# The slot table's one-hot matmuls with their operand sides exchanged, and a transpose behind them

## The chip, the cores and the metric

The kernel runs on one core of a Trainium2 chip: TensorE (matmuls), VectorE, ScalarE, GpSimd, SyncE (which issues most transfers) and 16 DMA engines. The metric is the device time of one execution in microseconds. The kernel before took 620.72 us in the median of three runs (619.73 to 621.04).

## What is computed

A small vision model: patches of 64 images become 37 tokens of 192 values each, an attention layer with relative positions is added, then a mixture of eight experts. The change lies in the routing ahead of the experts. Cut to what matters there:

```python
logits = xf @ Wg
topv, topi = jax.lax.top_k(logits, K)               # two experts for each token
w = jax.nn.softmax(topv, axis=-1)
order = jnp.argsort(-w[:, 0])                       # best first
e_ids = topi[order].reshape(T * K)
oh = jax.nn.one_hot(e_ids, E, dtype=jnp.int32)
pos = (jnp.cumsum(oh, axis=0) * oh).sum(-1) - 1     # place in the expert's list
keep = pos < cap
slot = jnp.where(keep, e_ids * cap + pos, E * cap)
buf = jnp.zeros((E * cap + 1, C), xf.dtype).at[slot].set(xf[tok_rep])
h = gelu(einsum('ecd,edh->ech', buf_e, W1) + b1)
out = einsum('ech,ehd->ecd', h, W2) + b2            # then weighted and added back to its token
```

There are 64 x 37 = 2368 tokens and 8 experts with room for 740 rows each. The kernel does not sort. It finds, for each expert, which tokens are in and where, and writes a **slot table**: for each of 8 x 6 tiles of 128 slots, which token sits in each slot. The rows of the tokens are then gathered by that table.

## The kernel before

Tokens are held as 22 groups (NG) of 111 partitions (G, three images of 37). The kernel has an image stage, an attention loop over pairs of groups, the routing stage (some 60 us, about 370 to 430 us in the trace), and a loop over the eight experts. There is no planner: each engine runs its own list in written order, and engines wait for one another by counting semaphores.

The end of the routing stage, with the lines of the profile:

- VectorE finds for each token and each of its two choices (j runs over 2 x 22 = 44 such columns) the tile and the row in the tile. L1632 makes `dest` (111 partitions x 48 tiles x 44, fp16): the token's number (its sign and an offset keep it in fp16) at the tile that it goes to, else 0. L1639 makes `onehot` (111 x 128 rows x 44, fp16) in two halves of 22 j each: 1 at the row in the tile. In both, j is the innermost dimension, so the values that belong to one j stand 44 elements apart. Each of the three instructions raises the semaphore `s_hot` by one.
- TensorE, L963, adds 44 matmuls in one PSUM bank. For each j, `onehot[:, :, j]` is the stationary side (111 x 128) and `dest[:, :, :, j]` the moving side (111 x 48). The sum is the table, 128 rows x 48 tiles, and the last matmul raises `s_tab`. A matmul with j below 22 needs only the first half of the one-hots.
- VectorE, L1644 to L1651, seven small steps on 128 x 48 values, turns the table into `gid`, the row number of each slot as an integer, and `valid`. L1651 raises `s_gid`.
- GpSimd, L1841, waits for `s_gid` and issues the indirect gathers of six tiles for expert 0 (`xe`), then those of expert 1 and 2.
- TensorE, behind the table, waits for `s_gid`, runs ten filler matmuls (`keep_warm`, L784, 128 x 128 by 512 columns, whose results are not used), then transposes each gathered tile as it lands (L974) with fillers between, and starts expert 0 (L1010). Another 20 fillers stand between the matmuls of L954, which count tokens, and L963.

In the trace `onehot`, `dest`, `tid` and `tvoid` are named `narrow`, and `tneg` and `tfold` are named `wide`, by the memory that they are cut from. `PS` is PSUM.

Of the kernel before, what the change touches and what calls it, by code (L numbers as in the profile page):

```python
# [23 lines left out]
E, HID = 8, 4 * D  # L24
# [22 lines left out]
NT = -(-CAP // 128)  # L47
# [51 lines left out]
def tile_rows(i):  # L99
    return min(128, CAP - 128 * i)  # L100


def build(nc, x, ln1_g, ln1_b, W_lin, b_lin, ln2_g, ln2_b, pos_embedding, cls_token,
# [7 lines left out]
    with ExitStack() as ctx:  # L111
        def sb(name, shape, dt=F32):
            return ctx.enter_context(nc.sbuf_tensor(name, shape, dt))
# [7 lines left out]
        def sem(name):  # L121
            return ctx.enter_context(nc.semaphore(name))

        PS = ctx.enter_context(nc.psum_tensor("PS", [128, 8, 512], F32))

        ident = sb("ident", [128, 128])
# [43 lines left out]
        def carve(memory):  # L170

            at = [0]

            def piece(parts, n, dt=F32):
                words = n if dt is F32 else n // 2
                a, at[0] = at[0], at[0] + words
                assert at[0] <= memory.shape[1]
                v = memory[0:parts, a:a + words]
                return v if dt is F32 else v.bitcast(dt)
            return piece  # L180
# [3 lines left out]
        piece = carve(wide)  # L184
        wraw = piece(128, 3 * NQKV).rearrange("p (b n) -> p b n", b=3)
        piece = carve(wide)
# [10 lines left out]
        piece = carve(wide)  # L197
# [4 lines left out]
        piece = carve(wide)  # L202
# [77 lines left out]
        piece = carve(narrow)  # L280
# [7 lines left out]
        piece = carve(narrow)  # L288
        onehot = piece(G, 2 * NG * 128, FP16).rearrange("p (n j) -> p n j", n=128)
# [3 lines left out]
        junk_a = piece(128, BY_ACT * G, BF16)  # L293
        mp_act = piece(128, BY_ACT * G)
        tid = piece(128, E * NT)
        tvoid = piece(128, E * NT)
        dest = piece(G, 2 * NG * E * NT, FP16).rearrange("p (e n j) -> p e n j", e=E, n=NT)

# [113 lines left out]
        s_hot = sem("slot_one_hots_ready")  # L412
        s_tab = sem("slot_table_psum")
# [27 lines left out]
        def bc(ap, shape):  # L441
            return ap.to_broadcast(shape)
# [201 lines left out]
        def _(pe):  # L644
# [4 lines left out]
            for c in range(PC):  # L649
                last = pe.matmul(PS[:, 6, 0:D], meanw[:, :], W_cen[:, c, :], start=(c == 0), stop=(c == PC - 1))  # L650
# [130 lines left out]
            def keep_warm(n, bank):  # L781

                for _ in range(n):
                    pe.matmul(PS[:, bank, 0:512], sums_to[:, 0, :], sums_to[:, 1:5, :].rearrange("p l m -> p (l m)"),  # L784
                              start=True, stop=True, skip_group_check=True)
# [123 lines left out]
            for m in range(HB):  # L909
                last = pe.matmul(PS[:, 6, m * R:(m + 1) * R], wrk[:, m * 128:(m + 1) * 128], pos_f[:, :],  # L910
                                 start=(m == 0), stop=(m == HB - 1), skip_group_check=True)
# [40 lines left out]
            for g in range(NG):  # L952
                one = ab[:, g:g + 1, :, :].rearrange("p a c e -> p a (c e)")
                last = pe.matmul(PS[0:G, 7, (g + 1) * width:(NG + 1) * width].rearrange("p (a c) -> p a c", c=width),  # L954
                                 onesb[:, :], bc(one, [G, NG - g, width]), start=False, stop=True,
                                 skip_group_check=True)
# [3 lines left out]

            for j in range(2 * NG):
                pe.wait_ge(s_hot, 2 + j // NG)
                last = pe.matmul(PS[:, 0, 0:E * NT], onehot[:, :, j], dest[:, :, :, j].rearrange("p e n -> p (e n)"),  # L963
                                 start=(j == 0), stop=(j == 2 * NG - 1))
            last.then_inc(s_tab, 1)
            def first_rows():

                pe.wait_ge(s_gid, 1)
                keep_warm(10, 7)
                for i in range(NT):  # L970
                    pe.wait_ge(s_one[i], 16)
                    n = tile_rows(i)
                    for k in range(2):
                        last = pe.transpose(PS[:, 2 * k + i // 4, 128 * (i % 4):128 * (i % 4) + n],  # L974
                                            xe[0:n, 0, i, k * 64:k * 64 + 128], ident[0:n, 0:n])
                    if i < NT - 2:
                        keep_warm(2, 7)
                last.then_inc(s_xep, 1)
                keep_warm(7, 7)
# [35 lines left out]
            def results(e):  # L1015
# [6 lines left out]
                for i in range(NT):  # L1022
# [14 lines left out]
                    last.then_inc(s_yp, 1)  # L1037

            first_rows()
            hidden(0, True)  # L1040
            expert_rows(1, 1, 0, 0)
# [203 lines left out]
        def _(dve):  # L1245
            v = nc.vector

            def ch(ins):

                dve.drain()  # L1250
# [28 lines left out]
            for c in range(PC):  # L1279
                last = v.tensor_scalar(W_cen[:, c, :], W_raw[:, c, :], g1[:, c:c + 1], None, ALU.mult)  # L1280
# [18 lines left out]
            for c in range(PC):  # L1299
                last = v.tensor_tensor(W_cen[:, c, :], W_cen[:, c, :], PS[:, 6, 0:D], ALU.subtract)  # L1300
# [339 lines left out]
                                bc(inrow[:, at].rearrange("p (a j) -> p a j", a=1), [G, 128, NG]), ALU.is_equal  # L1640
                                ).then_inc(s_hot, 1)
            dve.wait_ge(s_tab, 1)
            tab = PS[:, 0, 0:E * NT]
            ch(v.tensor_scalar(tneg[:, :], tab, -1.0, 0.0, ALU.mult, ALU.max))  # L1644
            v.tensor_scalar(tfold[:, :], tab, 0.0, float(FOLD), ALU.is_lt, ALU.mult)
            v.scalar_tensor_tensor(tvoid[:, :], tab, 0.0, slot_no[:, :, :].rearrange("p e n -> p (e n)"),
# [74 lines left out]
            with dve.Fori(0, E // 2 - 1) as i:  # L1721
                for p in (1, 0):
                    e = i * 2 + 2 - p
# [219 lines left out]
```

## Time and profile before

| | |
|---|---|
| median of three runs | 620.72 us (619.73 to 621.04) |
| the profiled execution | 620.7 us, its span 618.9 us |
| busy share of the span | TensorE matmul 88%, weight load 81%, VectorE 70%, ScalarE 42%, GpSimd 35% |
| mean granted TensorE clock | 0.939 of full speed (2.4 GHz) |
| the 44 table matmuls | 407.95 to 413.14 us |
| gid ready, first expert product | 414.58 us, 428.77 us |

The span is the time from the first to the last instruction of the program; the execution holds 1.8 us more around it. The busy shares are means over stages that are bound by different things, so they don't tell what the routing stage waits for. That is read from the chain of waits and the timeline of that stage. A matmul's duration in the trace holds its way through the array, which overlaps with the next one's, so the cost of one in a burst is the distance between starts. A granted clock of 0.50 is 1.2 GHz, and 1.00 is 2.4 GHz.

### The profile page before, as it was taken

How to read it: one execution, taken by the hardware profiler on the slowest of the kernel's cores; microseconds unless marked ns; L12 is line 12 of the kernel's file. 1: busy time of each engine (PE TensorE's matmuls, PEld its weight loads, DVE VectorE, ACT ScalarE, POOL GpSimd, SP SyncE). 2: the span in 40 equal slices, each digit the busy share in tenths (PEclk: the TensorE clock that was granted, in tenths of full speed). 3: DMA queues.
4: the chain of work that ended last, by engine and by line, in shares of the span. 5: the costliest groups of instructions: out<-in, count | busy, mean ns of one | idle time of the engine just before them, and what ended most of it. 6: DMA issues, size and time to landing. Idle time of an engine off the chain costs nothing.

```text
span 618.9 us, 12396 instructions
## 1 busy us (share of the span) xinstructions
PE 542.4 (88%) x4284; PEld 503.6 (81%) x4284; DVE 433.4 (70%) x1008; ACT 258.8 (42%) x415; POOL 218.2 (35%) x206
## 2 busy tenths in 40 slices
PE   4998477999999999999999796667999999999983
PEld 4997377989989999899899673344899999999982
DVE  6669676476776776777867757662778777777853
ACT  1333333242542443434425205402765685595560
POOL 0247320112012021021120105018587787787364
PEclk9999788799999999999999757869999999999997
DMA  8978632201202102112012008505375475466250
GB/s 198 227 170 246 171 80 63 46 14 39 51 0 51 34 16 51 26 25 51 11 39 51 2 4 226 141 1 134 82 165 134 94 170 136 92 145 149 21 166 32
DMA packets 61978, 54.96 MB, mean 89 GB/s; under 512 B 29174, under 2 KB 52534, under 8 KB 61152
## 3 DMA queue, kind: packets, MB, share of 16 engines
q1 hardware_dynamic: 52799, 46.04, 29.4%
q0 software_dynamic: 9152, 8.59, 8.3%
q8 instruction: 14, 0.23, 0.2%
q14 instruction: 13, 0.10, 0.1%
HBM read 39.32 MB, written 18.27 MB: 93 GB/s over the span
## 4 chain that ended last, share of the span: by engine, by line
PE 44%; DVE 13%; ACT 12%; issue 10%; SPq 9%; DMA 5%; POOL 3%; DVEq 2%; POOLq 0%; ACTq 0%
PE PS L1035 7%; PE PS L726 6%; PE PS L749 6%; ACT wide L1077 4%; PE PS L705 4%; PE PS L1033 4%; ACT hTh L1219 3%; PE PS L733 2%; DVE hTl L1686 2%; PE PS L742 2%; PE PS L740 2%; PE PS L741 2%; PE PS L1010 2%; SPq L496 2%; ACT b2w L1225 2%
## 5 line engine op out<-in xcount | busy, mean ns | idle before, releaser
L1737 POOL TENSOR_TENSOR rs<-ve,nhalf 111x1 f32<-111x1 f32 (+2 forms) x37 | 24.7, 668 | 276.4 <-DVE ve L1333 197.3
L1867 POOL DMA_INDIRECT running_sums<-ye,gid x42 | 73.4, 1747 | 34.8 <-DVE ye L1710 25.6
L1035 PE MATMUL PS<-w2hl,hTh 128*128 128x384 f32 (+1 forms) x288 | 82.8, 357 | 0.0
L1033 PE MATMUL PS<-w2hl,hTl 128*128 128x192 f32 (+1 forms) x288 | 73.5, 255 | 4.0 <-DVE hTl L1686 4.0
L1841 POOL DMA_INDIRECT xe<-routed_rows,gid x48 | 53.3, 1111 | 42.7 <-DVE gid L1651 28.5
L1010 PE MATMUL PS<-xeT,w1h 128*128 128x370 f32 x288 | 64.2, 331 | 2.1 <-issue 1.4
L1686 DVE TENSOR_TENSOR hTl<-hf,hTh 128x740 fp32r<-128x740 f32 x48 | 44.6, 928 | 24.7 <-ACT hTh L1219 23.5
L1033 PEld LDWEIGHTS PS<-w2hl,hTl 128*128 128x128 f32 (+1 forms) x288 | 53.7, 186 | 6.4 <-issue 5.6
L705 PE MATMUL PS<-xT,wh 128*128 128x222 f32 x264 | 46.8, 287 | 7.7 <-DVE xT L1347 7.7
L1035 PEld LDWEIGHTS PS<-w2hl,hTh 128*128 128x128 f32 (+1 forms) x288 | 52.9, 184 | 0.5
L1010 PEld LDWEIGHTS PS<-xeT,w1h 128*128 128x128 f32 x288 | 50.4, 188 | 2.8 <-issue 1.8
L1010 PE MATMUL PS<-xeT,w1l 128*128 128x370 f32 x192 | 48.0, 331 | 0.0
L705 PEld LDWEIGHTS PS<-xT,wh 128*128 128x128 f32 x264 | 37.7, 198 | 9.9 <-issue 9.8
L1216 ACT ACTIVATE hf<-PS,b1s 128x740 f32<-128x740 f32 x48 | 42.1, 877 | 6.3 <-PE PS L1010 3.9
L726 PE MATMUL PS<-wide 111*111 111x96 f32 x336 | 39.8, 283 | 1.0 <-DVE wide L1486 1.0
L674 PE MATMUL PS<-narrow 128*128 128x192 f32 x216 | 38.3, 328 | 2.7 <-ACT narrow L1060 2.5
L726 PEld LDWEIGHTS PS<-wide 111*111 111x111 f32 x336 | 37.9, 196 | 2.0 <-DVE wide L1486 1.1
L1365 DVE SCALAR_TENSOR_TENSOR wide<-PS,ind,wide 111x296 f32<-111x296 f32 x64 | 33.6, 525 | 6.1 <-DMA wide<-rel_scores 2.1
L674 PEld LDWEIGHTS PS<-narrow 128*128 128x128 f32 x216 | 34.7, 190 | 3.4 <-ACT narrow L1060 2.8
L705 PE MATMUL PS<-xT,wl 128*128 128x222 f32 x176 | 34.6, 279 | 0.0
L740 PE MATMUL PS<-woh,oTh 128*111 128x192 f32 x126 | 33.5, 266 | 0.9 <-DVE oTl L1395 0.9
L1090 ACT CAST oTh<-PS 128x666 fp32r<-128x666 f32 x21 | 15.1, 719 | 45.4 <-PE PS L733 45.4
(241 smaller groups left out, 1288.0 us busy)
## 6 DMA issues: line engine op xcount, KB each, us to landing
wide<-x SPq DMA_DIRECT2D x24, 288.0 KB, 13.3
w1r<-L_ffn_W SPq DMA_DIRECT2D x16, 384.0 KB, 4.9
rel_scores<-wide SPq DMA_DIRECT2D x66, 73.0 KB
w2r<-L_ffn_W SPq DMA_DIRECT2D x8, 576.0 KB, 4.6
w1r<-L_ffn_W SPq DMA_DIRECT2D x16, 192.0 KB, 4.5
wide<-rel_scores SPq DMA_DIRECT2D x22, 111.0 KB, 2.3
out<-running_sums SPq DMA_DIRECT2D x1, 1776.0 KB, 7.6
h_tokens<-narrow SPq DMA_DIRECT2D x24, 72.0 KB, 1.9
```

Source lines behind the costliest of these rows:

```text
L674: last = pe.matmul(PS[:, 4 + u % 4, 0:D], xTt[:, u % 2, c, :], W_cen[:, c, :], start=(c == 0), stop=(c == PC - 1))
L705: last = pe.matmul(PS[:, bank, (m % 2) * G2:(m % 2 + 1) * G2], lhsT, xT[:, b_, :], start=(nth == 0 and m % 2 == 0), stop=(nth == len(BLOCK ...
L726: last = pe.matmul(heads(4 - 2 * g, V)[:, j, :], pT[:, g, j * G:(j + 1) * G], v_sb[:, g, h * V:(h + 1) * V], start=(j % HB == 0), stop=Tru ...
L740: pe.matmul(PS[0:G, g, 0:D], oTh[:, g, at], woh[:, c, :], start=(c == 0), stop=False)
L749: last = pe.matmul(PS[0:G, 2 * g + n, 0:HB * V], xT[:, b_, g * G:(g + 1) * G], (wh, wl)[w][:, b_, at:at + HB * V], start=(nth == 0), stop= ...
L1010: last = pe.matmul(PS[:, hidden_bank(c) + n, 0:HALF], (w1h, w1l)[hl][:, b_, w], xeT[:, b_, n * HALF:(n + 1) * HALF], start=(nth == 0), sto ...
L1033: pe.matmul(PS[0:n, bank, 0:D], hTl[:, c, at], w2hl[:, c, 0, :], start=(c == 0), stop=False, skip_group_check=True)
L1035: last = pe.matmul(PS[0:n, bank, 0:2 * D], hTh[:, c, at], both(w2hl[:, c, :, :]), start=False, stop=(c == HC - 1), skip_group_check=True)
L1216: last = nc.scalar.activation(hf[:, c % 2, :].rearrange("p (a n) -> p a n", a=2), src, ACT.Gelu, bias=b1s[:, p, c:c + 1])
L1686: v.tensor_tensor(hTl[:, c, :], hf[:, c % 2, :], hTh[:, c, :].bitcast(F32), ALU.subtract).then_inc(s_hl, 1)
L1841: p_.indirect_dma_start(xe[0:r, p, n, :], None, xr_dram, bass.IndirectOffsetOnAxis(ap=gid[0:r, e, n:n + 1], axis=0), bounds_check=B * T - ...
L1867: p_.indirect_dma_start(sums, at, ye[0:r, e % 2, n, :], None, bounds_check=B * T + NT * 128 - 1, oob_is_err=True, compute_op=ALU.add).then ...
```

## The change

The two sides of the 44 matmuls are exchanged. `dest[:, :, :, j]` (111 x 48) is stationary and `onehot[:, :, j]` (111 x 128) is moving, so the table comes out as 48 partitions x 128 columns in bank 0. VectorE copies it to a new tile `tab_rows` (48 x 128, fp32) and raises `s_hot` to 4. TensorE waits for that and transposes `tab_rows` into bank 2, as 128 x 48, and raises `s_tab` to 2. VectorE waits for that, and its seven steps read bank 2 in place of bank 0. `tab_rows` is named `narrow` in the profile. Nothing else differs, but for the line numbers, which rise by 1 to 5.

```diff
+        tab_rows = piece(E * NT, 128)
...
             for j in range(2 * NG):
                 pe.wait_ge(s_hot, 2 + j // NG)
-                last = pe.matmul(PS[:, 0, 0:E * NT], onehot[:, :, j], dest[:, :, :, j].rearrange("p e n -> p (e n)"),
+                last = pe.matmul(PS[0:E * NT, 0, 0:128], dest[:, :, :, j].rearrange("p e n -> p (e n)"), onehot[:, :, j],
                                  start=(j == 0), stop=(j == 2 * NG - 1))
             last.then_inc(s_tab, 1)
+            pe.wait_ge(s_hot, 4)
+            pe.transpose(PS[:, 2, 0:E * NT], tab_rows[:, :], ident[0:E * NT, 0:E * NT]).then_inc(s_tab, 1)
...
             dve.wait_ge(s_tab, 1)
-            tab = PS[:, 0, 0:E * NT]
+            v.tensor_copy(tab_rows[:, :], PS[0:E * NT, 0, 0:128]).then_inc(s_hot, 1)
+            dve.wait_ge(s_tab, 2)
+            tab = PS[:, 2, 0:E * NT]
```

TensorE's list around the table, before (`sums_to` is what the fillers read, `xe` the gathered rows):

```order
L954 MATMUL PS<-wide,onesb 111x32
L954 MATMUL PS<-wide,onesb 111x16
L784 MATMUL PS<-sums_to 128x512 x20
L963 MATMUL PS<-narrow 128x48 x44
L784 MATMUL PS<-sums_to 128x512 x10
L974 MATMUL PS<-ident,xe 128x128 x2
```

and now:

```order
L955 MATMUL PS<-wide,onesb 111x32
L955 MATMUL PS<-wide,onesb 111x16
L785 MATMUL PS<-sums_to 128x512 x20
L964 MATMUL PS<-narrow 48x128 x44
L968 MATMUL PS<-ident,narrow 128x48
L785 MATMUL PS<-sums_to 128x512 x10
L977 MATMUL PS<-ident,xe 128x128 x2
```

The table's output turned from 128x48 to 48x128, and one transpose stands between it and the ten fillers.

VectorE's list from `dest` to the fourth of the seven steps, before:

```order
L1632 TENSOR_TENSOR narrow<-narrow,wide 111x2112
L1639 TENSOR_TENSOR narrow<-narrow,wide 111x128x22 x2
L1644 TENSOR_SCALAR wide<-PS 128x48
L1645 TENSOR_SCALAR wide<-PS 128x48
L1646 SCALAR_TENSOR_TENSOR narrow<-PS,slot_no 128x48
L1648 TENSOR_SCALAR valid<-PS 128x48
```

and now:

```order
L1635 TENSOR_TENSOR narrow<-narrow,wide 111x2112
L1642 TENSOR_TENSOR narrow<-narrow,wide 111x128x22 x2
L1646 COPY narrow<-PS 48x128
L1649 TENSOR_SCALAR wide<-PS 128x48
L1650 TENSOR_SCALAR wide<-PS 128x48
L1651 SCALAR_TENSOR_TENSOR narrow<-PS,slot_no 128x48
L1653 TENSOR_SCALAR valid<-PS 128x48
```

One copy of 48x128 stands between the one-hots and the seven steps.

## Rows read from the trace of the kernel before

**Rows 1.** Chain of waits, 405 to 430 us: start, us, engine and line.

```profile
406.36 1.55 DVE narrow L1639
...
407.95 5.19 PE PS L963 x44
...
413.17 0.21 DVE wide L1644
...
414.36 0.22 DVE gid L1651
...
415.51 0.33 POOL xe L1841
...
422.86 2.61 DMA xe<-routed_rows,gid
...
428.77 1.24 PE PS L1010 x6
```

**Rows 2.** Who waited for whom, 404 to 430 us: total us, times, longest.

```profile
POOL xe L1841 <- DVE gid L1651: 28.5, 1, 28.5
```

**Rows 3.** One line, L963: duration ns min/median/max, first and last start us.

```profile
L963 PE MATMUL PS<-narrow x44: 302/304/306, 408.0 to 412.8; 111*128 111x48 f16 x44
```

**Rows 4.** Timeline of TensorE's matmuls, 362 to 370 us: start, duration in us.

```profile
363.51 0.39 PE L741 MATMUL PS<-wol,oTh 128*111 128x192 f32 x1
...
366.49 0.39 PE L742 MATMUL PS<-woh,oTl 128*111 128x192 f32 x1
366.68 0.36 PE L898 MATMUL PS<-woh,oTh 128*37 128x192 f32 x1
...
369.40 0.36 PE L900 MATMUL PS<-woh,oTl 128*37 128x192 f32 x1
```

**Rows 5.** Busy us by engine in stretches; behind POOL granted clock, DMA share, GB/s.

```profile
363.30:366.60 3.30, 3.30 (x18) 3.30 (x19) 1.32 (x7) 0.00 (x0) 0.00 (x0) 0.50 0.00 0
366.70:369.50 2.80, 2.80 (x19) 2.73 (x18) 1.05 (x4) 0.00 (x0) 0.55 (x1) 0.50 0.00 0
397.20:400.40 3.20, 3.20 (x20) 2.10 (x19) 0.96 (x4) 0.45 (x1) 0.00 (x0) 0.50 0.00 0
400.60:404.00 3.40, 3.40 (x16) 1.37 (x14) 3.02 (x8) 0.00 (x0) 0.00 (x0) 1.00 0.01 2
404.10:407.20 3.10, 0.00 (x0) 0.00 (x0) 3.02 (x3) 0.00 (x0) 0.00 (x0) 1.00 0.00 0
407.40:413.20 5.80, 5.18 (x44) 4.92 (x44) 2.06 (x3) 0.00 (x0) 0.00 (x0) 0.50 0.02 3
414.65:417.50 2.85, 2.85 (x7) 1.01 (x8) 2.46 (x3) 0.00 (x0) 1.81 (x1) 0.50 0.00 0
417.60:425.50 7.90, 4.70 (x22) 1.83 (x20) 0.00 (x0) 0.00 (x0) 6.48 (x7) 1.00 0.25 66
```

**Rows 6.** Groups of instructions, VectorE, whole span: busy us, mean ns, idle before.

```profile
L1306 DVE COPY cB<-PS 128x192 f32<-128x192 f32 x1 | 0.4, 352 | 0.0
...
L1644 DVE TENSOR_SCALAR wide<-PS 128x48 f32<-128x48 f32 x1 | 0.2, 208 | 3.7 <-PE PS L963 3.7
```

**Rows 7.** One line, L888, columns as in rows 3.

```profile
L888 PE MATMUL PS<-ident,wide x6: 298/298/321, 361.4 to 362.0; 37*128 37x37 f32 x6
```

**Rows 8.** One line, L733, 360.1 to 361.3 us, columns as in rows 3.

```profile
L733 PE MATMUL PS<-ident,wide x6: 390/393/446, 360.1 to 361.1; 111*128 111x111 f32 x6
```

**Rows 9.** Chain of waits, 394.3 to 396.3 us, columns as in rows 1.

```profile
394.62 0.17 DVE last_in L1605
...
394.84 0.38 PE PS L945
...
395.24 0.34 DVE wide L1610
```

**Rows 10.** One line, L784, 400.6 to 403.9 us, columns as in rows 3.

```profile
L784 PE MATMUL PS<-sums_to x16: 379/379/431, 400.4 to 403.7; 128*128 128x512 bf16 x16
```

**Rows 11.** One line, L1639, columns as in rows 3.

```profile
L1639 DVE TENSOR_TENSOR narrow<-narrow,wide x2: 1620/1620/1621, 406.3 to 407.8; 111x2816 f16<-111x2816 f16 x2
```

## The prediction

> **What bounds the kernel now.** I read the chain of waits first, since a change of a few matmuls counts only if it lies on what ends last. In the routing stage the chain runs in one line: VectorE makes the first half of the one-hots (406.36), TensorE runs the 44 table matmuls from 407.95 for 5.19 us, VectorE takes the table at 413.17 and has the gather indices (gid) at 414.36, GpSimd gathers the routed rows from 415.51, the last gather's transfer runs from 422.86 for 2.61, and the experts' first product starts at 428.77 [rows 1]. The reader should see that no other engine stands between these steps. The view of who waited for whom says the same from the other side: GpSimd sat idle for 28.5 us until gid [rows 2]. So a microsecond on the way from one-hots to gid is a microsecond of the whole time.
>
> Then I read what one of the 44 matmuls costs. A single one lasts 304 ns, the first starts at 408.0, the last at 412.8 [rows 3]; the chain's 5.19 us less 0.304 for the last, over 43 steps, is **0.1136 us a step** (0.112 from the rounded starts). The moving side is 48 columns, the stationary side 128. To see which of the two sets the step I took a place in the trace where the stationary width changes and the moving width does not: with 111 stationary columns and 192 moving, 16 steps go from 363.51 to 366.49, 0.186 us each; with 37 stationary and the same 192 moving, 17 steps go from 366.68 to 369.40, 0.160 each [rows 4], both at a granted clock of 0.50 [rows 5]. So a wide stationary side sets the step, and with a narrow one the moving side does, at 0.160/192 = 0.833 ns a column, which is the 1.2 GHz level. In the table matmuls 48 moving columns would be 0.040 us by that price; the step of 0.1136 is the load of 128 stationary columns, 0.887 ns each.
>
> **The change, part by part.** *The 44 matmuls.* Stationary goes from 128 to 48 columns: 48 x 0.887 = 0.043 us. Moving goes from 48 to 128: 128 x 0.833 = 0.107 us. The larger sets the step: 0.107. The burst is then 43 x 0.107 + 0.31 = 4.91 us against 5.19, **-0.28**. What is moved streams through the array in a step nearly as long as the load that it replaces, so little is won. Both tiles keep 44 values side by side for each column, so neighbours in a column sequence lie 88 bytes apart, before and after. The trace has no wide moving operand of that kind. Its cost is bounded from above by the 48 columns that now hide in 0.1136 us, 2.37 ns a column, which would make a step of 0.303 and a burst of 13.3 us (+8.2); from below by the steps at the upper clock, where 512 moving columns go at (403.7 - 400.4)/15 = 0.22 us [rows 10], 0.055 for 128 (the nearest row of a stream without a stationary bound). The nearest row to it is the stationary side of these same matmuls, read with the same 88 bytes at 0.887 ns a column: 0.1136 a step, which saves nothing. I take 0.107 to 0.114, and 0.107 for the sum.
>
> Here a rule speaks against the change. The trace shows 0.887 ns for a stationary column 88 bytes apart, against the 0.833 of a moving column without gaps [rows 3, 4], 6% more. The Trainium skill (Advanced Engine Details and Errata, SBUF Cachelines) says that reads that touch a different 16-byte line each time pay a penalty, and names no figure. By that rule 128 such columns on the moving side could cost more than the 48 did; by the row they cost 6% more at most. I go by the row and keep the rule as a rival below.
>
> *The copy.* VectorE copies 48 partitions x 128 columns out of PSUM. A pass over 48 PSUM columns takes 208 ns, a copy of 192 columns 352 [rows 6]: 1 ns a column, so 128 columns are 0.29 us. It is on the path, before it nothing can start. The handover from TensorE to it is the one that L1644 has today.
>
> *The transpose.* One fp32 transpose, stationary 48 x 128, moving 48. The nearest row is the 37 x 128 one at the same clock, 321 ns for the longest of its run [rows 7]; 111 x 128 took 446 at most [rows 8], and a lone 128 x 111 one with 128 moving 0.38 in the chain [rows 9]. I take 0.34 and keep 0.32 to 0.45. The handovers around it are read from that lone transpose: VectorE's result at 394.62 + 0.17, TensorE's start at 394.84, its end at 395.22, VectorE's next at 395.24 [rows 9], 0.05 and 0.02. Behind TensorE's new wait are queued only the ten filler matmuls and the expert transposes, which wait for gid and the gathers anyway; on VectorE the whole gid computation waits, which is the path itself.
>
> Added together: 0.29 + 0.05 + 0.34 + 0.02 = **+0.70**, bounds 0.68 to 0.81. The rest (seven small VectorE steps, now read from another PSUM bank, and the gathers) keeps its cost.
>
> *The sum.* The profiled execution took 620.7 us (span 618.9 and 1.8 around it), the median of the three runs is 620.72, so both bases agree. 620.7 - 0.28 + 0.70 = **621.1**. With a step of 0.1136 and the longer transpose it is 621.5. A measurement of this kernel can tell about 0.2%, 1.24 us, from no change; the forecast lies inside that.
>
> **Rivals.** *The clock rises in the burst.* Granted TensorE clock was 0.50 (1.2 GHz) for all of 407.4 to 413.2. It had been 1.00 (2.4 GHz) from 400.6 to 407.2 and fell after TensorE had done nothing from 404.1 on; in 397.2 to 400.4 and in 414.65 to 417.5 wide matmuls ran back to back at 0.50, and the stretch behind each has 1.00 [rows 5]. The 5.2 us of 48-column matmuls did not bring it up; 128 moving columns fill nearly the whole step and might. If it rises 2.9 us after the start, as it did for the filler that began at 414.65, 27 of the 44 are done and 17 save 0.107 - 0.055 each, 0.88 us in all: 621.1 - 0.9 = 620.2. If it did not fall at all ahead of the burst, the second half of the one-hots, ready at 407.8 + 1.62 = 409.4 [rows 11], holds matmul 23 back, and the burst ends about 410.9, 2.2 us earlier: 620.7 - 2.2 + 0.7 = 619.2. Against it: the copy and the transpose remain, and one burst of this kind in the trace stayed at 0.50.
>
> *The strided moving side is slow.* This ends on the other side. If each moving column takes two steps of the 1.2 GHz clock, 1.67 ns, a step is 0.213 and the burst 43 x 0.213 + 0.31 = 9.5 us: +4.3 + 0.7, 625.7. It decides from a step of 0.126 us on, where the loss passes 1.24 us. For it: no row shows a wide moving operand with gaps. Against it: the stationary read with the same gaps at 0.887 ns.
>
> *It isn't on the path.* If something else released the gathers within a fraction of a microsecond of gid, the sum would vanish: 620.7. The 28.5 us of idle GpSimd [rows 2] speak against it.
>
> **How the numbers follow.** Forecast (step 0.107 to 0.114, clock at 0.50) 0.60; clock higher in some of the burst 0.20; slow moving side 0.13; off the path 0.07. Slower by over 0.2%: 0.13 and a tail of the forecast, 0.05, together 0.18. Faster by over 0.2% needs the whole burst at the upper level, a quarter of the second case, 0.05. Within: 0.77. The range runs from 619.8 (most of the clock case) to 622.5 (the forecast's bounds and the spread of the runs shown, 1.3 us), and leaves out the slow stream and the fastest clock case.
>
> **What would show it.** In the profile after: the starts of the first and last table matmul 4.6 us apart; a 48 x 128 copy of about 0.29 us; one transpose of 0.32 to 0.45; gid about 0.4 us later behind the one-hots than now (8.00 us from 406.36 to 414.36), and the gathers later by the same. A first-to-last distance over 5.4 us makes the moving side the culprit; under 4 us with a clock above 0.50 is the second case. If the steps are as said and the time still moves by over 1.24 us, the path behind gid is where I was wrong.

## The result, and the profile after

The changed kernel took **629.58 us** (median of 6 runs, 627.14 to 632.05) against 620.55 of the kernel before (6 runs, 619.73 to 621.04): a ratio of 1.0147, interval 1.0122 to 1.0173, some 9 us slower. The forecast was 621.1, inside the range of no change.

The loss sits in one place. The chain of waits of the changed kernel, with the same columns as [rows 1]:

```profile
407.45 1.26 DVE narrow L1635
408.71 1.55 DVE narrow L1642
...
410.30 13.13 PE PS L964 x44
...
423.46 0.29 DVE narrow L1646
...
423.80 0.35 PE PS L968
...
424.17 0.21 DVE wide L1649
...
425.36 0.22 DVE gid L1656
...
426.52 0.33 POOL xe L1846
...
433.86 2.62 DMA xe<-routed_rows,gid
...
439.79 1.95 PE PS L1013 x10
```

The 44 matmuls take 13.13 us where they took 5.19. Everything behind them is as forecast: 0.29 for the copy, 0.35 for the transpose, 0.05 and 0.02 for the handovers, and the seven steps, the gathers and the expert's start keep the distances of [rows 1]. GpSimd's wait for gid is 10 us longer than in [rows 2], though this profile's routing stage also began later. Who waited for whom:

```profile
POOL xe L1846 <- DVE gid L1656: 38.5, 1, 38.5
```

To compare profiles whose routing stages start at different times I use the distance from the start of dest to the end of gid. Before, dest starts at 405.10:

```profile
405.10 1.26 DVE narrow L1632
```

and gid ends at 414.36 + 0.22 [rows 1], so 9.48 us. Now it is 425.58 - 407.45 = 18.13, **8.65 us more**: 13.13 - 5.19 = 7.94 for the burst, 0.71 for copy, transpose and handovers. On 620.55 that makes 629.2, and 629.58 was measured. (The profiled execution itself is the longest of the six, 632.05: it reached dest 2.3 us later than the one before did.)

One matmul of the burst and the two new steps, as in [rows 3] (duration ns min/median/max, first and last start, shapes):

```profile
L964 PEld LDWEIGHTS PS<-narrow x44: 167/178/190, 410.3 to 422.6; 111*48 111x48 f16 x44
L964 PE MATMUL PS<-narrow x44: 482/483/504, 410.3 to 422.9; 111*48 111x128 f16 x44
```

```profile
L1646 DVE COPY narrow<-PS x1: 283/283/283, 423.5 to 423.5; 48x128 f32<-48x128 f32 x1
```

```profile
L968 PE MATMUL PS<-ident,narrow x1: 339/339/339, 423.8 to 423.8; 48*128 48x48 f32 x1
```

A step is (422.9 - 410.3)/43 = **0.293 us**, for 128 moving columns 2.29 ns each. Before it was 0.1136 for 48 moving columns, 2.37 ns each. By the moving side's price the two steps agree; by the price that the prediction used (0.833 ns a moving column, the rest the load) they don't.

The clock is no part of the loss. Stretches of the changed kernel, as in [rows 5]:

```profile
397.20:401.00 3.80, 3.80 (x23) 3.47 (x24) 0.00 (x0) 1.19 (x2) 0.00 (x0) 0.50 0.00 0
...
406.60:410.20 3.60, 0.11 (x1) 0.00 (x0) 3.53 (x4) 0.00 (x0) 0.00 (x0) 1.00 0.00 0
410.40:423.30 12.90, 12.90 (x44) 7.63 (x44) 1.38 (x1) 0.00 (x0) 0.00 (x0) 0.50 0.01 1
```

The burst ran at 0.50 (1.2 GHz), as before; the clock had been 1.00 while TensorE did next to nothing from 406.6 to 410.2, and fell as the burst began. The 12.9 us in which matmuls were always in flight did not bring it back.

### The profile page after: what moved, and what is told of

It reads as the page before. It is cut to its first block, busy times and chain, and to the rows that moved or that the text cites. A ratio compares the mean times of both kernels' runs of the same rounds, so it can differ in the third digit from the quotient of the medians.

```text
span 630.1 us, 12399 instructions
## 1 busy us (share of the span) xinstructions
PE 557.1 (88%) x4285; PEld 511.8 (81%) x4285; DVE 433.6 (69%) x1009; ACT 258.8 (41%) x415; POOL 218.3 (35%) x206
## 4 chain that ended last, share of the span: by engine, by line
PE 45%; DVE 13%; ACT 12%; issue 10%; SPq 10%; DMA 5%; POOL 3%; DVEq 2%; POOLq 0%; ACTq 0%
PE PS L1038 7%; PE PS L727 6%; PE PS L750 6%; ACT wide L1080 4%; PE PS L706 4%; PE PS L1036 4%; ACT hTh L1222 3%; PE PS L734 2%; PE PS L964 2%; PE PS L741 2%; PE PS L743 2%; PE PS L742 2%; SPq L497 2%; DVE hTl L1691 2%; PE PS L1013 2%
## 5 line engine op out<-in xcount | busy, mean ns | idle before, releaser
L675 PE MATMUL PS<-narrow 128*128 128x192 f32 x216 | 39.7, 337 | 2.6 <-ACT narrow L1063 2.6
L675 PEld LDWEIGHTS PS<-narrow 128*128 128x128 f32 x216 | 36.4, 198 | 2.8 <-ACT narrow L1063 2.8
L1013 PEld LDWEIGHTS PS<-xeT,w1l 128*128 128x128 f32 x192 | 34.1, 188 | 0.0
```

Of the source, the lines that this page charges most:

```text
L675: last = pe.matmul(PS[:, 4 + u % 4, 0:D], xTt[:, u % 2, c, :], W_cen[:, c, :], start=(c == 0), stop=(c == PC - 1))
L1013: last = pe.matmul(PS[:, hidden_bank(c) + n, 0:HALF], (w1h, w1l)[hl][:, b_, w], xeT[:, b_, n * HALF:(n + 1) * HALF], start=(nth == 0), sto ...
```

## The experiments

Theories. **Gaps**: a moving column that lies 88 bytes from its neighbour costs 2.3 ns, and this set the step in both kernels. **Load** (the prediction's): the load of the stationary side set the old step, and something about the new 48-wide load sets the new one. **Moving fp16 at all** costs 2.3 ns a column at the lower clock.

### after_pairs: the gaps closed on the moving side of the changed kernel

```diff
-        onehot = piece(G, 2 * NG * 128, FP16).rearrange("p (n j) -> p n j", n=128)
+        onehot = piece(G, 2 * NG * 128, FP16).rearrange("p (b n q) -> p b n q", n=128, q=2)
...
-                last = pe.matmul(..., dest[:, :, :, j].rearrange("p e n -> p (e n)"), onehot[:, :, j],
+                last = pe.matmul(..., dest[:, :, :, j].rearrange("p e n -> p (e n)"), onehot[:, j // 2, :, j % 2],
```

> The changed kernel, with the one-hots laid out in pairs: 22 blocks of 128 columns x 2 values, so that neighbouring moving columns lie 4 bytes apart in place of 88. Stationary side (48 columns, 88 bytes apart), copy and transpose are as in the changed kernel. Gap theory (a moving column 88 bytes from its neighbour costs 2.3 ns, whichever kernel): the step falls from 0.293 us to about 128 x 0.833 ns = 0.107, the burst from 13.1 to 4.9 us, the time from 629.6 to about 621.4. Load theory (a 48-wide stationary side with gaps loads slowly): the step stays 0.293, time 629.6. Theory that any fp16 moving column costs 2.3 ns at the lower clock: also 0.293.

The step as the line's view shows it:

```profile
L964 PE MATMUL PS<-narrow x44: 308/308/353, 410.4 to 415.0; 111*48 111x128 f16 x44
```

(415.0 - 410.4)/43 = 0.107 us. In the burst only the distance between moving columns was changed; stationary side, data, type, output and granted clock (0.50 from 410.4 to 415.2) are the same, and the step fell from 0.293 to what 128 columns take at 1.2 GHz. That is the gap theory's number, and neither of the others'. The time was another matter: 627.32 us, ratio 1.0114 (1.0092 to 1.0136), where 621.4 was expected. The edit had also put the table of row numbers that the one-hots are compared with into pairs, and GpSimd's timeline shows what that cost (start, duration):

```profile
377.63 31.01 POOL L1833 IOTA narrow<- 111x5632 f16 x1
```

against this in the kernel before:

```profile
381.50 5.47 POOL L1829 IOTA narrow<- 111x5632 f16 x1
```

31 us in place of 5.5, until 408.64, so the first one-hots started 4.9 us after the end of dest (402.54 + 1.26 = 403.80, then 408.68). This profile's execution was the fastest of the five, 623.92; how long the others waited isn't shown. It is a fault of the experiment, mended in after_pairs_b.

### after_fours and after_elevens: other distances

The same edit with q=4 (8 bytes) and with q=11 (22 bytes; here the row numbers were already held once, as in after_pairs_b).

> As after_pairs with blocks of 128 columns x 4 values: neighbouring moving columns 8 bytes apart. Gap theory in the form that only wide gaps cost: 0.107 us a step, as with pairs. Gap theory in the form that cost grows with the distance: between 0.107 and 0.293. Load theory: 0.293.

> The changed kernel with the one-hots in 4 blocks of 128 columns x 11 values: neighbouring moving columns 22 bytes apart (4 bytes gave 0.107 us a step, 8 bytes 0.117, 88 bytes 0.293). If the cost comes with every column that lies in another 16-byte line: as with 88 bytes, 0.293. If it grows with the distance: about 0.14 to 0.16.

```profile
L964 PE MATMUL PS<-narrow x44: 293/296/339, 408.7 to 413.8; 111*48 111x128 f16 x44
```

```profile
L964 PE MATMUL PS<-narrow x44: 413/417/460, 408.3 to 418.5; 111*48 111x128 f16 x44
```

(413.8 - 408.7)/43 = 0.119 us at 8 bytes and (418.5 - 408.3)/43 = 0.237 at 22. A moving column costs 0.83 ns at 4 bytes, 0.93 at 8, 1.85 at 22 and 2.29 at 88. The bursts at 4, 22 and 88 bytes ran at 0.50, but in that at 8 bytes the clock changed, and the step did not:

```profile
409.30:412.50 3.20, 3.20 (x30) 3.20 (x28) 0.77 (x1) 0.00 (x0) 0.00 (x0) 0.50 0.02 5
412.70:414.00 1.30, 1.30 (x13) 1.18 (x10) 0.00 (x0) 0.00 (x0) 0.00 (x0) 1.00 0.00 0
```

```profile
L964 PE MATMUL PS<-narrow x27: 293/296/299, 409.2 to 412.3; 111*48 111x128 f16 x27
```

```profile
L964 PE MATMUL PS<-narrow x11: 293/297/300, 412.6 to 413.8; 111*48 111x128 f16 x11
```

At 0.50 it is (412.3 - 409.2)/26 = 0.119 us, at 1.00 (413.8 - 412.6)/10 = 0.12. So 8 bytes look nearly free only beside the price of the lower clock: by [rows 10], bf16 columns without gaps went at 0.22 us for 512 at 1.00, 0.055 for 128, less than half.

The expectation of 0.14 to 0.16 at 22 bytes, for a cost that grows with the distance, was wrong, and so was 0.293 for one that is the same for every new line. The Trainium skill (Advanced Engine Details and Errata, SBUF Cachelines) puts the penalty where each access falls in another 16-byte line and two hits on a line absorb it. At 0.50 the runs agree as far as 8 bytes, two columns to a line, cost a tenth and 22 bytes more than double; at 1.00 two hits did not absorb it. Counted by such lines the two runs come to one price: 64 lines in 0.119 us and 128 in 0.237 are 1.85 ns a line each, and at 4 bytes 32 lines would take 0.059, hidden behind the 0.107 of the clock. This reading is argued from two runs and not tested further, and that 88 bytes cost another quarter (2.29) is not in it.

The times of the single runs, 622.4 at 8 bytes and 627.3 at 22, follow the steps: from dest to gid they are 0.97 and 6.25 us longer than before. Their dest starts at 405.75 and 405.30 against 405.10 before, and 620.7 + 0.65 + 0.97 = 622.3, 620.7 + 0.20 + 6.25 = 627.2.

### after_warm: the gaps at the upper clock

```diff
-            keep_warm(20, 1)
+            keep_warm(34, 1)
```

> The changed kernel with 34 fillers in place of 20 ahead of the table matmuls, so that TensorE is busy until shortly before the burst and the granted clock is still 1.00 when it starts. If the gaps bind at the memory's side: the step stays near 0.293 us at clock 1.00, time 629 to 630. If the 2.3 ns a column are steps of TensorE's own clock: 0.147 us in the part at 1.00, and the time falls by up to 6 us.

Stretches of the burst (columns as in [rows 5]), then the line's matmuls in the first and in a later stretch:

```profile
406.50:408.00 1.50, 1.46 (x5) 0.97 (x6) 1.50 (x1) 0.00 (x0) 0.00 (x0) 1.00 0.00 0
...
412.00:419.60 7.60, 7.60 (x27) 4.29 (x25) 0.00 (x0) 0.00 (x0) 0.00 (x0) 0.50 0.00 0
```

```profile
L964 PE MATMUL PS<-narrow x5: 484/484/507, 406.5 to 407.7; 111*48 111x128 f16 x5
```

```profile
L964 PE MATMUL PS<-narrow x22: 483/484/484, 411.6 to 417.7; 111*48 111x128 f16 x22
```

At 1.00 four steps take 407.7 - 406.5, some 0.3 us each, with the same duration of 484 ns; at 0.50 it is (417.7 - 411.6)/21 = 0.290. Doubling TensorE's clock changed nothing, so the 2.3 ns are not steps of that clock. With the runs on the distance it points to the reading of the moving operand; which part of the way from memory sets it isn't shown. The single run took 628.48 us. It also shows that the clock case of the prediction could not have helped this burst, since the step is the same at either level. (The fillers ended 1.1 us ahead of the burst, and the clock still fell to 0.50 within it.)

### before_destpairs: the gaps closed on the moving side of the kernel before

```diff
-        dest = piece(G, 2 * NG * E * NT, FP16).rearrange("p (e n j) -> p e n j", e=E, n=NT)
+        dest = piece(G, 2 * NG * E * NT, FP16).rearrange("p (b e n q) -> p b e n q", e=E, n=NT, q=2)
...
-                last = pe.matmul(PS[:, 0, 0:E * NT], onehot[:, :, j], dest[:, :, :, j]...
+                last = pe.matmul(PS[:, 0, 0:E * NT], onehot[:, :, j], dest[:, j // 2, :, :, j % 2]...
```

> The kernel before with dest laid out in pairs: the 48 moving columns lie 4 bytes apart in place of 88; the stationary one-hots keep their 88 bytes. Gap theory: 48 x 2.3 ns = 0.110 us is what sets the old step of 0.1135; it falls to what the load of 128 stationary columns takes, at most 0.107 if a stationary column costs 0.833 ns. Load theory of the prediction (0.887 ns for each stationary column): the step stays 0.1135. L1632, which writes dest, may take longer than its 1.26 us.

This is the run that separates the two readings of the *old* step. The stationary one-hots are untouched.

```profile
L963 PE MATMUL PS<-narrow x44: 233/238/268, 408.5 to 411.5; 111*128 111x48 f16 x44
```

```profile
408.50:411.70 3.20, 3.15 (x44) 3.03 (x44) 1.52 (x1) 0.00 (x0) 0.00 (x0) 0.50 0.02 5
```

```profile
405.09 1.95 DVE narrow L1632
...
408.54 3.16 PE PS L963 x44
...
412.92 0.22 DVE gid L1651
```

The burst is 3.16 us where it was 5.19, at the same granted clock of 0.50; first to last start is (411.5 - 408.5)/43 = 0.070 us, in which one wait for the second half of the one-hots is contained. A load of 128 stationary columns with 88-byte gaps therefore takes 0.070 at most. It did not set the old step of 0.1136: the 48 moving columns did, at 2.37 ns. The expectation had put that load at 0.107 or less; it is a third below that.

dest takes 1.95 us in place of 1.26, and from dest to gid it is 413.14 - 405.09 = 8.05 us, 1.43 less than before. The single run took 619.76 us against 619.91, which is too few to tell. For its time it was run again:

> before_destpairs again, for its time: dest 0.69 us longer, the burst 2.0 us shorter than in the kernel before (3.15 against 5.18), so 1.3 us under the kernel before on the same chip, a ratio of 0.998. If the steps of the burst were not on the path: 1.000.

620.06 us against 620.52 in the medians, ratio over all runs 0.9976 (0.9961 to 0.9992). By the ratio it is 1.5 us faster (0.5 to 2.4), by the medians 0.5; the profile's 1.43 lies inside the interval.

### after_pairs_b: the exchange without the gaps

```diff
-        row_no = piece(G, 2 * NG * 128, FP16).rearrange("p (n j) -> p n j", n=128)
+        row_no = piece(G, 2 * 128, FP16).rearrange("p (b n q) -> p b n q", n=128, q=2)
```

and the comparison spreads it over the blocks.

> after_pairs once more, with the row numbers held once as 128 x 2 values and spread over the blocks, since the table of row numbers in after_pairs took GpSimd 31 us and held the one-hots back. Gap theory: the step is 0.107 us, the one-hots follow dest directly, and the time is that of the kernel before plus copy and transpose less a little: 619.9 + 0.7 - 0.3 = 620.3, 621 at most. If something else of the exchange costs time (the wait, the transpose, the gathers): up to 629.

```profile
403.87 1.26 DVE narrow L1635
...
406.71 4.95 PE PS L964 x44
...
411.69 0.29 DVE narrow L1645
...
412.03 0.35 PE PS L968
...
413.60 0.22 DVE gid L1655
```

```profile
406.71:411.65 4.94, 4.94 (x44) 4.71 (x44) 1.48 (x1) 0.00 (x0) 0.00 (x0) 0.50 0.01 3
```

The burst is 4.95 us at a granted clock of 0.50, the copy 0.29, the transpose 0.35, and from dest to gid it is 413.82 - 403.87 = 9.95 us, 0.47 more than before. The time was 620.89 against 621.09, ratio 1.0005 (0.9989 to 1.0020). This is the kernel that the prediction's prices describe (it put the burst at 4.91 us and the whole at 0.4 more), and within what can be measured it costs what they said. So all but about half a microsecond of the 9 comes from the gaps on the moving side.

### before_allpairs and before_destfours_cut: the gaps closed on both sides of the kernel before

before_allpairs is the kernel before with dest and one-hots in pairs. before_destfours_cut has dest in fours, one-hots in pairs, and cuts the one-hots 32 to 12:

```diff
-            for k in range(2):
-                at = slice(k * NG, (k + 1) * NG)
+            for a, z in ((0, 16), (16, 22)):
...
-                pe.wait_ge(s_hot, 2 + j // NG)
+                pe.wait_ge(s_hot, 2 + (j >= 32))
```

> The kernel before, both dest and the one-hots in pairs (4 bytes apart on both sides). before_destpairs left a step of 0.065 us. If the 88 bytes of the stationary one-hots set that: the step falls to 0.040 to 0.055 (48 moving columns at 0.833 ns are 0.040), though the first 22 then wait for the second half of the one-hots. If the load of 128 columns takes 0.065 whatever the distance: 0.065. The time: dest takes 0.7 us more, the burst about 2.5 us less: 618.1.

> The kernel before with dest in fours (8 bytes apart, which may cost VectorE less than pairs), one-hots in pairs, and the one-hots cut 32 to 12 in place of 22 to 22, so that little is left for TensorE when the last of them is ready. Expected: dest 1.6 us (1.26 before, 1.95 in pairs); the burst ends 12 x 0.05 + 0.25 = 0.85 us behind the one-hots, where it ended 3.7 us behind them before: 619.9 + 0.35 - 2.85 = 617.4.

Chain and line of before_allpairs:

```profile
406.14 1.94 DVE narrow L1632
408.08 3.00 DVE narrow L1638 x2
...
411.12 1.08 PE PS L963 x22
...
413.41 0.22 DVE gid L1650
```

```profile
L963 PE MATMUL PS<-narrow x44: 214/214/222, 409.6 to 412.0; 111*128 111x48 f16 x44
```

The last 22 matmuls take 1.08 us; less 0.214 for the last, over 21 steps, that is 0.041 each, the price of 48 columns at 1.2 GHz; the granted clock of the burst was 0.50. The stationary side's gaps did cost something (0.070 to 0.041), but it no longer shows: the burst now waits for VectorE, whose one-hots stand in the chain for 3.00 us in its place. From dest to gid 413.63 - 406.14 = 7.49 us, 1.99 less than before; the time 619.14 against 621.09, ratio 0.9967 (0.9951 to 0.9983), 2.05 us. Chain of before_destfours_cut:

```profile
405.28 1.52 DVE narrow L1632
...
409.02 2.26 PE PS L963 x44
...
412.49 0.22 DVE gid L1650
```

412.71 - 405.28 = 7.43 us, 2.05 less than before. Its burst of 2.26 us begins with the first 32 one-hots and ends soon after the last 12. The time was 618.28 against 621.09, ratio 0.9962 (0.9938 to 0.9986), where 2.5 us less were expected, and in a second set

> before_destfours_cut again, for its time: dest 0.26 us longer, the burst 2.24 us in place of 5.18 and its start 0.66 us later behind the first one-hots, so 2.0 us under the kernel before on the same chip, a ratio of 0.9967. If the steps of the burst were not on the path: 1.000.

619.73 against 620.52, ratio 0.9986 (0.9970 to 1.0001). The ratios make 2.4 and 0.9 us, and the second interval reaches no change; the profile's 2.05 lies inside the first interval and just outside the second (at most 1.9). It is not told apart from before_allpairs by its time.

## Why the prediction was wrong

- **That the stretch is on the path, one to one: right.** 8.65 us more from dest to gid, about 9 in the time; 1.43 and 1.99 less, 1.5 and 2.05 in the time by the ratios.
- **Copy 0.29, transpose 0.34, handovers 0.07: right.** 283 and 339 ns and the same handovers, 0.71 in sum against 0.70.
- **What sets the old step: wrong, and this is the step that failed.** The prediction read that "the step of 0.1136 is the load of 128 stationary columns, 0.887 ns each". It reasoned from [rows 4], where the step fell as the stationary side narrowed, and those rows are of 4-byte operands, 111 and 37 columns wide, with no gaps on either side; by them a stationary column costs 0.186/111 = 1.68 ns, which already is not 0.887. The load of 128 fp16 columns is a different one: 0.070 us at most with gaps (before_destpairs), 0.041 at most without (before_allpairs).
- **The price of a moving column: the term that was mis-sized.** 0.833 ns was taken and 2.29 measured; the burst was put at 4.91 us and took 13.13. The prediction had stated the other reading as its upper bound, 2.37 ns a column and 13.3 us, "the 48 columns that now hide in 0.1136 us". They did not hide. They were the step, and the bound was the answer.
- **The rival with a slow moving side: right in kind, too small.** It was priced at two steps of the clock, 0.213 us and 625.7, with a chance of 0.13. The step was 0.293, and not in steps of TensorE's clock, as after_warm shows. The range of 619.8 to 622.5 left it out.
- **The rule that spoke against the change was set aside by a row that doesn't show it.** The 6% that the prediction gave as the price of gaps, 0.887 against 0.833 ns, compared a stationary column that was not what the step waited for.
- **The clock rival: did not occur.** The burst ran at 0.50, and after_warm at 1.00 gave the same step. In after_fours the clock did rise within the burst, and there too the step stayed.

## What to carry to other kernels

Where two operands of a step could each set its length, rows of another shape and type don't decide which; price the change by both readings, and if one of them is many times dearer, the range has to reach it or an experiment on one side has to come first. Before a matmul operand goes from the stationary to the moving side, look at how far apart its columns lie: at a granted clock of 0.50, 4 bytes cost nothing and 8 a tenth, while 22 and 88 cost two to nearly three times as much. At 1.00 the step at 8 bytes was no shorter, and 4 bytes were not run. Layouts in pairs or fours kept VectorE's one-hots as fast as they were (3.15 us for both parts in after_pairs_b and in after_fours, 3.16 before) while they closed the gaps for TensorE; dest took longer, as said below.

## What the runs showed of the hardware that was not expected

A load of 128 fp16 columns is faster than one of 111 bf16 columns. In the kernel before, at 0.50, L954's matmuls with 64, 48, 32 and 16 moving columns are set by their 111-wide load; the timeline has the first and the last of them at

```profile
398.36 0.44 PE L954 MATMUL PS<-wide,onesb 111*111 111x64 bf16 x3
```

```profile
398.64 0.24 PE L954 MATMUL PS<-wide,onesb 111*111 111x16 bf16 x1
```

so (398.64 - 398.36)/3 = 0.093 us a step, 0.84 ns a column, against 0.041 or less for 128 columns in before_allpairs. The Trainium skill (TensorE: Matmul & The Clock Gate, Weight-path perf modes) says that a fast weight load is on when the number of weights is 128 and the type is not fp32. The two numbers agree with it, though type and width differ at once, and it would have told that the old step need not be the load. The trace's records of the loads in the kernel before differ too: those of L963 read 4 pieces of 32 columns, those of L954 one of 111.

The 2.3 ns of a moving column 88 bytes from the next are the same at both clock levels (after_warm), and so are the 0.93 ns at 8 bytes (after_fours).

The length of the innermost run matters to some writers too. VectorE's write of dest took 1.26 us with runs of 44 values, 1.52 with runs of 4 and 1.95 with runs of 2; GpSimd's table of row numbers, 5632 values, took 5.5 us with runs of 44 and 31 with runs of 2. The one-hots in pairs, whose output has no gaps, cost VectorE nothing.
